# Layer 3 begun inside layer 2's last feed-forward group, and layer 3's second projection in seven block products

## The reference, cut to what matters

```
# layer 2, second half: T = 4096 tokens, F = 1024
x = x + g_mlp * (gelu(modulate(layernorm(x)) @ W1 + b1) @ W2 + b2)

# layer 3
nx = x * rsqrt(mean(x*x) + 1e-5) * weight * (1 + scale[b]) + shift[b]     # per batch b
q, k, v = nx @ wq + bq, nx @ wk + bk, nx @ wv + bv                        # 16 heads of 16
q, k = q*cos + rotate_half(q)*sin, k*cos + rotate_half(k)*sin
x = x + softmax(q @ k.T / 4) @ v @ wo + bo                                # inside each batch
nx = adaptive rms norm of x, with the second set of weights
x = x + (gelu(nx @ w_gate) * (nx @ w_up)) @ w_down                        # 256 -> 1024 -> 256
```

## Time and profile before

| | |
|---|---|
| median of 3 runs | 2682.57 us (2680.64 to 2686.27) |
| the profiled execution's own time | 2682.27 us |
| its span, first to last instruction | 2680.5 us, so 1.8 us lie around it |
| PE busy | 2495.6 us (93%) |
| DVE busy | 1739.7 us (65%) |
| ACT busy | 1193.7 us (45%) |
| POOL busy | 497.1 us (19%) |
| layer 2's last group ends, layer 3 begins | about 2087 to 2129 us |
| layer 3's attention | about 2129 to 2357 us |
| layer 3's feed-forward | about 2357 to 2677 us |

### The profile page before, as it was taken

How to read it: one execution, slowest core, us unless ns; L and a number is a source line. 1 busy time by engine, 2 the same in 40 slices (tenths; PEclk the granted TensorE clock), 3 DMA queues, 4 the chain that set the end, 5 groups by cost and what they waited for, 6 DMA issues and landing times.

```text
span 2680.5 us, 63359 instructions
## 1 busy us (share of the span) xinstructions
PE 2495.6 (93%) x25441; PEld 1941.6 (72%) x25441; DVE 1739.7 (65%) x3894; ACT 1193.7 (45%) x2460; POOL 497.1 (19%) x476
## 2 busy tenths in 40 slices
PE   6999699999999956998999999998999799999999
PEld 5787366666666645887888888887666588778888
DVE  4888687788788766554455555545555399965554
ACT  4886355565565512432332333333334377632322
POOL 1323000110010014654011011102000266600000
PEclk9999899999999957999999999999999799999999
DMA  6000000000000043444200000000000133300000
GB/s 217 3 3 3 20 24 23 31 23 23 27 28 23 17 107 98 133 108 106 78 0 0 0 0 0 0 0 1 1 1 1 32 110 116 103 9 8 17 16 16
DMA packets 72161, 102.22 MB, mean 38 GB/s; under 512 B 10880, under 2 KB 50304, under 8 KB 71488
## 3 DMA queue, kind: packets, MB, share of 16 engines
q1 hardware_dynamic: 65856, 91.46, 10.6%
q0 software_dynamic: 6144, 8.56, 1.7%
HBM read 67.20 MB, written 32.80 MB: 37 GB/s over the span
## 4 chain that ended last, share of the span: by engine, by line
PE 79%; DMA 7%; DVE 6%; issue 2%; ACT 2%; POOL 2%; SPq 1%; DVEq 0%; ACTq 0%; POOLq 0%
PE psW L323 17%; PE psW L316 9%; PE psS L1624 8%; PE psP L1477 8%; DMA rotated<-work 6%; PE psP L435 4%; PE psS L1616 4%; PE psP L442 4%; PE psO L1477 4%; PE psW L546 3%; PE psO L415 3%; PE psS L382 3%; PE psO L347 2%; PE psP L398 2%; PE psW L1477 2%
## 5 line engine op out<-in xcount | busy, mean ns | idle before, releaser
L323 PE MATMUL psW<-r,work 128*128 128x512 f32 x1024 | 481.5, 604 | 1.0 <-DVE work L812 1.0
L1336 POOL TENSOR_TENSOR work<-work 128x512 f32<-128x512 f32 x128 | 132.0, 1042 | 1132.5 <-DVE work L846 1132.5
L323 PEld LDWEIGHTS psW<-r,work 128*128 128x128 f32 x1024 | 180.5, 191 | 162.4 <-issue 156.8
L316 PE MATMUL psW<-work,r 128*128 128x128 f32 x2048 | 244.3, 278 | 1.3 <-DVE work L812 1.0
L316 PEld LDWEIGHTS psW<-work,r 128*128 128x128 f32 x2048 | 235.4, 193 | 4.2 <-DVE work L812 1.4
L1624 PE MATMUL psS<-r,work 128*128 128x256 f32 x992 | 217.3, 379 | 0.0
L1624 PEld LDWEIGHTS psS<-r,work 128*128 128x128 f32 x992 | 187.8, 190 | 25.3
L1247 ACT ACTIVATE work<-work 128x512 f32<-128x512 f32 x128 | 80.1, 626 | 278.0 <-DVE work L825 278.0
L1879 ACT ACTIVATE work<-psP 128x512 f32<-128x512 f32 x64 | 38.2, 597 | 296.1 <-PE psP L1477 296.1
L810 DVE TENSOR_TENSOR work<-psW,tab 128x256 f32<-128x256 f32 x64 | 27.0, 421 | 185.0 <-PE psW L309 185.0
L546 PE MATMUL psW<-work,r 128*128 128x128 f32 x1024 | 138.4, 291 | 7.1 <-ACT work L1140 6.3
(11 more groups left out here) (335 smaller groups left out, 5192.0 us busy)
## 6 DMA issues: line engine op xcount, KB each, us to landing
r<-in_l_fc SPq DMA_DIRECT2D x16, 1024.0 KB, 6.8
rotated<-work SPq DMA_DIRECT2D x60, 256.0 KB
work<-mod_rows SPq DMA_DIRECT2D x64, 128.0 KB, 2.9
work<-rotated SPq DMA_DIRECT2D x30, 256.0 KB
r<-in_l_w SPq DMA_DIRECT2D x2, 3072.0 KB, 14.6
x<-in_x SPq DMA_DIRECT2D x8, 512.0 KB, 9.6
gather_table<-work SPq DMA_DIRECT2D x32, 128.0 KB, 1.8
moe_sum<-work SPq DMA_DIRECT2D x32, 128.0 KB, 1.7
```

Of the source, the lines that this page charges most:

```text
L316: ins = nc.tensor.matmul(ps[:, q * P:(q + 1) * P], w[:, k, lo + q * P:lo + (q + 1) * P], L.hT[:, k, :], start=(k == 0), stop=(k == KC - 1))
L323: ins = nc.tensor.matmul(ps[:, 0:width], L.hT[:, k, :], w[:, k, lo:lo + width], start=(k == 0), stop=(k == KC - 1))
L1336: nc.gpsimd.tensor_tensor(E, E, halves(L.rs)[i].unsqueeze(2).broadcast_to([P, 8, N]), ALU.mult).then_inc(L.s[f"prob{i}"].sem, 1)
```

## The change

1. **Layer 3's head.** Its first turns, queries, keys and values now stand inside layer 2's last group on PE (`pe_l3_head`, parts 0, 1 and 2); DVE normalises tiles 0 to 2 there; no engine but PE waits for `l2ff`, and PE only before the first scores. The buffers of layer 3 are laid behind those of layer 2 (`take_behind`), the two `turned` buffers lie over layer 2's hidden values, so SP's first two reads wait for its last `f_y`.
2. **The roots.** DVE's Newton steps for layer 3 are gone. POOL takes them with the power function: tiles 0 to 23 in layer 2's last group, 24 to 31 in layer 3's first tile.
3. **The second projection.** `result` of layer 3's feed-forward becomes `second`: 14 parts of four products of 128 rows by 128 columns, a seven-product scheme. The weight sums come from POOL (`pool_second_sums`), five input sums from DVE, eight copies out of PSUM from ACT; six block sums and the addition into x from DVE. The modulation of the next group's input is taken apart into two halves, put between them. POOL's sums of layer 3's gate and up weights are spread over layer 2's groups.

```diff
 def dve_ff(v, ch, Q):                                        # hidden_two, layer 2
+                if Q.kind == "l2" and not ahead:
+                    v.wait_ge(su["root"], 7)
+                    dve_norm(v, ch, L[3], 0)
...
+                if Q.kind == "l2" and not ahead:
+                    dve_norm(v, ch, L[3], 1)
...
             if Q.kind == "l2":
+                dve_norm(v, ch, L[3], 2)
+                dve_sines(v, L[3], 0)
                 add(NG - 1)
                 measure(NG - 1)
+        def pe_l3_head(pe, part):
+            if part == 0:
+                turn_x(0, 0)                                  # behind hidden of the last group
+            elif part == 1:                                   # between result's two halves
+                pe.wait_ge(L[3].ready, 16 * L[3].loads)
+                qk(0)
+                turn_x(1, 0)
+            else:                                             # ahead of back(NG - 1)
+                values(0, 2)
+                pe.wait_ge(su["mask4"], 1)
+                rotate(0)
+                bias_product()
+                qk(1)
+                turn_x(2, 1)
 def dve_narrow(v, ch, L):
-            if rotary:
-                dve_rstd(ch, rms=True)
-                for n in range(3):
-                    dve_norm(v, ch, L, n)
-                sines(0)
...
 the gpsimd stream
-            after(g, Q["l2"].s["f_h"], 1)
             g.wait_ge(ld["l3"], 80)
-            pool_weight_sums(g, Q["l3"], 0, 0)
-            following(g, "l2ff")
+            pool_weight_sums(g, Q["l3"], 0, 0, lambda i: after(g, Q["l2"].s["f_h"], 2 + i))
+            pool_second_sums(g, Q["l3"], 0, 0)
+            after(g, Q["l2"].s["f_h"], NG)
+            pool_rms(g, 0, 0, 24)
             pool_narrow(g, L[3])
 the sync stream
                 after(sp, L[3].s["rsin"], n - 1)
+                if n < 4:
+                    after(sp, Q["l2"].s["f_y"], NG)
                 sp.dma_start(rows_of(L[3].turned[u]), rotated[u, :, 8:24, :]).then_inc(back.sem, 16)
 def pe_ff(pe, Q):
+            def second(t, u):
+                def part(bank, h, at, w, first=True):
+                    for k in range(4):
+                        ins = nc.tensor.matmul(bank[:, 0:P], h[:, k, at:at + P], w[:, k, :], ...)
+                    ins.then_inc(done, 1)
...
+                for m in range(2):
+                    if m == 0:
+                        after(pe, *Q.summed(t, "left", 1))
+                    after(pe, *Q.part(t - 1, "y21", m))
+                    part(bank_a[m], low, P * m, b11)
+                after(pe, *Q.summed(t, "left", 3))
+                for m in range(2):
+                    part(bank_c[m], high, P * m, b21)
+                after(pe, Q.s["f_sum"], 8)
+                after(pe, *Q.summed(t, "s1", 1))
+                for m in range(2):
+                    part(bank_d[m], s1, P * m, t1)
+                after(pe, *Q.summed(t, "s2", 0))
+                for m in range(2):
+                    after(pe, *Q.part(t, "q1", m))
+                    part(bank_a[m], s2, P * m, t2, False)
+                after(pe, *Q.summed(t, "s3", 0))
+                for m in range(2):
+                    after(pe, *Q.part(t, "q2", m))
+                    part(bank_a[m], low, 256 + P * m, t3, False)
+                after(pe, *Q.summed(t, "s4", 0))
+                for m in range(2):
+                    after(pe, *Q.part(t, "q3", m))
+                    part(bank_a[m], high, 256 + P * m, t4, False)
+                    after(pe, *Q.summed(t, "y22", m))
+                    part(bank_d[m], s4, P * m, b22, False)
 def dve_ff(v, ch, Q):                                        # end of hidden_l3
                 left_product(t, 3)
+                after(v, *Q.summed(t, "right", 2))
+                first_sum(t)
                 c12(t, 3)
+                if ahead:
+                    modulate(t + 1, 0)
                 right_product(t, 3)
+                after(v, *Q.summed(t, "right", 3))
+            def second(t, u, ahead):
+                second_sums(t)                                # s1 (second half), s2, s3, s4
+                if ahead:
+                    block(t, "y11", 0)
+                    block(t, "y11", 1)
+                    modulate(t + 1, 1)
+                    block(t, "y22", 0)
+                    block(t, "y22", 1)
+                    mix_input()
...
+                block(t, "y12", 0)
+                block(t, "y12", 1)
+                finish(t, u)                                  # the addition into x
 def act_ff(a, Q):
+            def second(t):
+                for name, product, r, lo in (("q1", "b", 0, 0), ("q2", "d", 0, P), ("q3", "e", 2, P), ("y21", "g", 2, 0)):
+                    for m in range(2):
+                        after(a, *Q.product(t, product, m))
+                        nc.scalar.activation(Q.y[:, r + m, lo:lo + P], psS[:, 512 * m:512 * m + P], ACT.Copy
+                                             ).then_inc(s["f_part"].sem, 1)
```

More of the change, by code:

```diff
@@ L636, in pe_narrow @@
                 turn_x(4, 2)
+                following(pe, "l2ff")
+            else:
+                pe.wait_ge(L.ready, 16 * L.loads)
+                turn_x(0, 0)
+                qk(0)
+                turn_x(1, 0)
+                values(0, 2)
+                bias_product()
+                qk(1)
+                turn_x(2, 1)
+                values(1, 3)
             pe.wait_ge(su["bias"], 1 if L.li == 0 else 2)
@@ L1634, in step @@
                 hidden(t, u, ahead)
-                result(t, u, late_group)
+                if t < Q.seconds:
+                    second(t, u)
+                else:
+                    result(t, u, late_group)
                 if late_group:
@@ L1670, in dve_ff_modulate @@
             for k, ps in enumerate((psW0, psW1)):
+                if half not in (None, k):
+                    continue
                 if Q.kind == "moe":
@@ new lines, in first_sum, with block @@
+            def first_sum(t):
+                low, high = Q.hid[:, 0:4, :], Q.hid[:, 4:8, :]
+                s1 = Q.mix2[0]
+                nc.vector.tensor_tensor(s1[:, 0:2, :], low[:, 0:2, 256:512], high[:, 0:2, 256:512], ALU.add
+                                        ).then_inc(Q.s["f_summed"].sem, 1)
+            def block(t, name, m):
+                out, bank, product, part = {
+                    "y11": (Q.y[:, m, 0:P], psP, "a", "q1"),
+                    "y22": (Q.y[:, 2 + m, P:D], psO, "c", "q3"),
+                    "y12": (Q.y[:, m, P:D], psO, "f", "q2")}[name]
+                after(v, *Q.product(t, product, m))
+                after(v, *Q.part(t, part, m))
+                nc.vector.tensor_tensor(out, bank[:, 512 * m:512 * m + P], out, ALU.add
+                                        ).then_inc(Q.s["f_summed"].sem, 1)
@@ L1852, in step @@
                     hidden_two(t, ahead)
+                if t < Q.seconds:
+                    second(t, u, ahead)
+                    return
                 if ahead:
@@ L1935, in step @@
                     gate(t, 3, 1)
+                    second(t)
                     return
```

204 lines of the change are left out of this document (153 added, 51 removed).

## The result

The changed kernel takes **2655.93 us** (median of 4 runs, 2650.93 to 2657.93) against 2684.42 for the kernel before beside it (4 runs, 2680.64 to 2687.49): ratio 0.9889, interval 0.9874 to 0.9905. The forecast was 2657.6, with a range of 2651 to 2669. A second set of runs of the same kernel gives 2658.2. As a gain, 24.7 us were forecast; the medians differ by 28.5 and the profiled executions by 26.2.

A forecast was written before the change was run, and what follows sets the result against it. The prediction took SP's serial chain to pace layer 3's attention, started late by the boundary's serial chain, and PE to bound the feed-forward. Terms of 18.9 and 5.8 us made 24.7 off 2682.27: 2657.6 us, range 2651 to 2669.

The forecast's parts named there:

- What bounds the kernel: Layer 3's attention: SP's serial write, wait, read chain paces it at 7.10 us a tile; feed-forward: PE alone.
- Term 1: Layer 3's head: SP's first write starts 20.8 us earlier, less 1.9 for the clock: 18.9 us, bounds 13.8 and 20.8.
- The list: Layer 3's head: new PE order laid over old row durations at full clock, `biased(2)` ending at 2104.4 against 2125.24.
- The 1.9 us taken off for the clock: Layer 3's head: one `qk` at half clock; rival that the clock falls at once: 2662.7 us, chance 0.24.
- The roots: Layer 3's Newton roots moved to POOL: 1.8 to 7.1 us for 24 columns, hidden, costed at nothing.
- The moved weight sums read what nobody else touches: nothing.: POOL's sums of layer 3's weights, moved within layer 2's feed-forward: costed at no effect.
- Term 2: Layer 3's second projection: 13.1 us a group against 13.82, 5.8 us saved in all, bounds -6.9 and 10.0.
- the stall: Layer 3's second projection: PE waits about 0.5 us a group for DVE's sums, ahead of the products into psO.
- The rival of the weight loads: Layer 3's second projection: weight loads no longer hidden, kernel slower at 2723 us, or 2698 by 81 ns a pass; chance 0.03.
- The sum: Whole kernel: 18.9 + 5.8 = 24.7 us off the profiled 2682.27, giving 2657.6 us; chance 0.50.

The follow-up runs named there:

- the writes ahead: Changed kernel with SP issuing the write of tile n+1 before waiting for that of tile n: 2654.16 us, ratio 0.9885; with the other DVE order too, 2649.24 us.
- the addition late: Changed kernel with the next group's first modulation's addition and its second modulation moved behind sum s2 on DVE in layer 3's feed-forward: 2651.32 us, ratio 0.986.

## Why the prediction was right, and where it was not

- **What bounds the kernel.** The head's gain reached SP's first write one for one, and the attention followed it less 3.3 us. That the attention ends a fixed time after SP's first write was right but for that; that SP's chain alone sets its pace was half of the truth. In the earlier trace rows the chain gives 7.1 us a tile, but the engines settle at 7.05 by themselves, as the runs with the writes ahead show. Two limits lay 0.05 us apart, and the prediction names one.
- **Term 1**, 18.9 us. The list was right to 0.1 us at full clock: 20.8 forecast, 20.9 measured. The 1.9 us taken off for the clock were wrong: it stayed at 1.00, and the list without them was the right end of the bounds. In the earlier trace rows the clock fell behind 0.18 us of work in 3.3 and behind 1.72 in 4; with the head behind layer 2 it fell behind 0.84 and behind 1.71 in 4; the changed kernel had 12.52 in 20. No row at hand had such a stretch, so the term could not be read off and was a choice inside the bounds.
- **The roots**, costed at nothing: right, 5.25 us with 8 us to spare.
- **"The moved weight sums read what nobody else touches: nothing."** This is the step that failed, by 7.1 us. It asked who reads the data, not who shares the engine's way to it, and it never looked at where the old burst stood. In the old timeline four instructions that take 0.41 alone took 0.94 and three times 2.4; the 4.33 us of PE's wait for L796 would have led there.
- **Term 2**, 5.8 us: 5.1 in the stage, 5.3 against the kernel with the head alone. The group (13.16 against 13.1) and the stall (0.42 against 0.5, at its place) are right; six periods give 0.65 each against 0.7, and the last group 0.92 against 0.95. What is short of the forecast is the first group, 0.3 instead of 0.7; it overlaps the end of the attention, and its length differs between traces by more than that, so that 5.1 instead of 5.8 is within what the stage varies by (318.6 to 320.6 us in the five traces with the old projection). The Trainium skill's spacing of 81 ns a pass ("TensorE: Matmul & The Clock Gate", "Back-to-back issue gap") would make, as an estimate, 18.1 us a group. The trace does not agree: it has 12.5 without the stall, 56 ns a pass. The rival of the weight loads is out.
- **The sum.** 24.7 were forecast, 26.2 came in the profile. Of the difference, +7.1 are the sums, +2.0 the head with its clock, -3.3 the attention, -0.7 the projection, and -3.6 the stretch upstream. The total is right partly by luck, because errors of both signs met.

## What to carry to other kernels

Cut both traces at the same events and compare stage by stage: a total within 2 us hid an error of 7 and one of 3. Ask of every moved instruction on GpSimd what VectorE does at its old place and at its new one, since one can hold the other up without touching the same data (8.21 us instead of 1.75 here). When a serial chain is named as the pace, look at how fast the engines behind it would go without it, because only the difference can be gained.

The version with the addition late and the buffers shifted is the fastest median measured here, 2646.17 us, 9.8 us under the changed kernel. Each was measured against the kernel before beside it, and by these ratios the shift brings nothing (0.9861 against 0.986 without it); the late addition alone, 2651.32, is the part that is shown by its stage.

## What the runs showed of the hardware

- Four TENSOR_SCALAR steps of VectorE on 128 x 256 float32 in SBUF take 1.75 us alone and 8.21 beside four GpSimd additions and subtractions of 128 x 1024, which themselves stay at 2.34 to 2.36; each step ends 0.15 us behind one of them. A VectorE operation with an operand in PSUM beside them keeps its 0.69.
- GpSimd's power function takes 1.05 us for 4 columns, 1.67 for 8 and 4.20 for 24: by these three an estimate of 0.16 a column and 0.4 fixed.
- The granted clock of TensorE stayed at 1.00 over 20 us with 12.52 busy in gaps of 1.1 to 2.2 us, and with the head behind layer 2 it fell behind 4 us with 0.84 of work and behind 4 us with 1.71.
- Products of 128 x 128 x 128 in float32, each with its own weights, run at 0.223 us each in an unbroken stretch of 56.
- With the source buffer of a DMA and two others 128 bytes further on, SP's 30 waits came to 147.7 us instead of 157.6, in one trace each. The cause is not shown.
